# Two sixteenths of the relation weights moved from TensorE to VectorE, and five target one-hots made in one comparison

## What is computed

```python
def rgcn_gate_layer(x, row, col, edge_type, basis, att, gate_w, root, bias):
    w = jnp.einsum('rb,bio->rio', att, basis)      # att 2x30, basis 30x512x512
    x_j = x[col]
    msgs = []
    for r in range(2):
        gate = jax.nn.sigmoid(x_j @ gate_w[r, :, 0])
        msgs.append(gate[:, None] * x_j @ w[r])
    msg = jnp.where((edge_type == 0)[:, None], msgs[0], msgs[1])
    agg = jax.ops.segment_sum(msg, row, num_segments=x.shape[0])
    return agg + x @ root + bias
xn = _layernorm(x)
h = relu(rgcn_gate_layer(xn, ..., basis1, ...)); gnn = rgcn_gate_layer(h, ..., basis2, ...)
x = x + gnn + mix(xn)
x = x + ffn(_layernorm(x))
```

## Time and profile before

| | us |
|---|---|
| three runs | 502.63, 501.56, 502.21 (median 502.21) |
| the profiled execution | 500.15 |
| its span, first to last instruction | 498.4 |
| PE busy | 456.5 (92%) |
| DVE busy | 218.0 (44%) |
| POOL busy | 177.7 (36%) |
| ACT busy | 166.8 (33%) |
| mean granted TensorE clock | 0.987 of full speed |

### The profile page before, as it was taken

How to read it: one execution, slowest core, us unless ns; L and a number is a source line. 1 busy time by engine, 2 the same in 40 slices (tenths; PEclk the granted TensorE clock), 3 DMA queues, 4 the chain that set the end, 5 groups by cost and what they waited for, 6 DMA issues and landing times.

```text
span 498.4 us, 7432 instructions
## 1 busy us (share of the span) xinstructions
PE 456.5 (92%) x2602; PEld 321.5 (65%) x2602; DVE 218.0 (44%) x527; ACT 166.8 (33%) x365; POOL 177.7 (36%) x201
## 2 busy tenths in 40 slices
PE   2799799979999999798999999999999999999993
PEld 2344356768765665466667788777777877775772
DVE  5779981322262626553313002333002658853445
ACT  2799763322220111831205004225006360133320
POOL 3101200055230541199061790622404625940522
PEclk9999999999999999999999999999999999999986
DMA  5999999868999978964910816040002193999646
GB/s 126 380 427 417 429 423 362 345 249 311 369 399 412 383 256 322 422 256 179 315 47 2 250 44 252 1 108 1 5 1 64 42 336 101 272 343 359 209 156 196
DMA packets 38788, 119.27 MB, mean 239 GB/s; under 512 B 7050, under 2 KB 7111, under 8 KB 30302
## 3 DMA queue, kind: packets, MB, share of 16 engines
q1 hardware_dynamic: 33406, 111.30, 59.8%
q0 software_dynamic: 3360, 3.86, 3.2%
q10 hardware_dynamic: 1984, 3.61, 1.9%
HBM read 103.92 MB, written 14.82 MB: 238 GB/s over the span
## 4 chain that ended last, share of the span: by engine, by line
PE 75%; DMA 7%; issue 5%; DVE 3%; ACT 3%; POOL 2%; SPq 2%; DVEq 1%; POOLq 0%; ACTq 0%
PE ps L1637 14%; PE ps L1639 13%; PE ps L1638 13%; PE ps L1661 9%; PE ps L1996 9%; DMA ring<-in_L_gnn_basis_dram 4%; PE ps L1722 3%; DMA y_dram<-ybuf 2%; PE ps L2131 2%; PE ps L2121 2%; PE ps L1841 2%; ACT h_tmp L1374 1%; PE ps L1645 1%; POOL piece_lo L746 1%; DMA got<-y_dram,slot_u 1%
## 5 line engine op out<-in xcount | busy, mean ns | idle before, releaser
L1661 PE MATMUL ps<-ring,sel_att 128*32 128x512 f32 x512 | 66.0, 602 | 6.5 <-DMA ring<-in_L_gnn_basis_dram 3.0
L1637 PE MATMUL ps<-piece_hi,ht_hi 128*125 128x512 f32 x140 | 56.1, 401 | 0.8 <-PE ps L1639 0.6
L1097 DVE SCALAR_TENSOR_TENSOR u_lo<-ps,gates,u_hi 125x512 fp32r<-125x512 f32 x20 | 15.0, 751 | 94.1 <-ACT u_hi L1520 94.1
L1638 PE MATMUL ps<-piece_lo,ht_hi 128*125 128x512 f32 x140 | 55.1, 394 | 0.0
L1639 PE MATMUL ps<-piece_hi,ht_lo 128*125 128x512 f32 x140 | 55.1, 394 | 0.0
L745 POOL CAST piece_hi<-piece_raw 128x512 fp32r<-128x512 f32 x28 | 19.8, 707 | 91.9 <-issue 53.7
L746 POOL TENSOR_TENSOR piece_lo<-piece_raw,piece_hi 128x512 fp32r<-128x512 f32 x28 | 37.8, 1350 | 13.4 <-issue 11.2
L947 DVE TENSOR_SCALAR oh_n<-iota_n,keys 125x626 f16<-125x626 f16 x100 | 37.8, 378 | 8.1 <-PE ps L1722 6.1
L1996 PE MATMUL ps<-u_hi,cf 125*125 125x512 f32 x100 | 39.9, 399 | 1.3 <-PE ps L1639 1.3
L1996 PE MATMUL ps<-u_lo,cf 125*125 125x512 f32 x100 | 39.4, 394 | 0.0
L1722 PE MATMUL ps<-oh_n,oh_m 125*128 125x313 f16 x200 | 31.4, 314 | 4.0 <-DVE oh_m L948 3.9
(11 more groups left out here) (334 smaller groups left out, 929.7 us busy)
## 6 DMA issues: line engine op xcount, KB each, us to landing
ring<-in_L_gnn_basis_dram SPq DMA_DIRECT2D x64, 1024.0 KB, 8.0
w_home<-in_L_ffn_W_sp_dram SPq DMA_DIRECT2D x27, 256.0 KB, 6.5
rel_dram<-stag SPq DMA_DIRECT2D x16, 256.0 KB, 7.9
w_raw<-rel_dram SPq DMA_DIRECT2D x8, 512.0 KB, 6.8
w_fq<-in_L_ffn_W_fq_dram SPq DMA_DIRECT2D x2, 2048.0 KB, 10.7
y_dram<-ybuf ACTq DMA_DIRECT2D x13, 256.0 KB, 4.5
piece_raw<-in_L_mix_Wkqv_dram SPq DMA_DIRECT2D x3, 1024.0 KB, 9.4
x_dram<-stag SPq DMA_DIRECT2D x1, 3072.0 KB
```

The costliest lines, as they stand in the source:

```text
L1097: dve.scalar_tensor_tensor(out=u_lo[l][:, t, :], in0=ps[0:TP, u_bank(i), :], scalar=gates[:, t, r:r + 1], in1=u_hi[l][:, t, :].bitcast(F32 ...
L1637: pe.matmul(target, a_hi, b_hi, start=first, stop=False, skip_group_check=skip)
L1638: pe.matmul(target, a_hi, b_lo, start=False, stop=False, skip_group_check=skip)
L1661: last = pe.matmul(ps[32 * c:32 * c + 32, rel_bank(ch), :], sel_att[:, ch // CHUNKS, g].rearrange("p r q -> p (r q)"), ring[slot][:, c * D ...
```

## The change

Two things change.

First, PE makes only 14 chunks (56 parts). The last two chunks of the second layer, 128 of its 512 input rows, are summed on DVE. For that SP loads the rows of those two chunks in 60 DMAs of 128 KB, into the four `ring` buffers, 64 partitions each (`load_for_vector`): bases 0 to 15 as the last four parts are used on PE, bases 16 to 29 as DVE uses up the first. DVE adds them up in `stag` (`sums`), two relations x 30 bases = 60 instructions of 128 x 512, both inputs and the output in SBUF; `SUMS` gives the order, the two relations in turn for bases 0 to 15, then relation 0 and relation 1 one after the other for the rest. They stand in DVE's list like this: two ahead of each of the five `W2` tiles, three ahead of `gate_row`, six behind it, two behind each `u_lo` of relation 0, and the remaining 31 between relation 0 and relation 1. Each sum waits for its buffer, and for the sum before it on the same relation. The storing and reading back of the second layer's weights is split by relation. ACT no longer copies chunks 14 and 15. SP loads `root2` and `x_again` at other places in its list.

Second, the five `oh_m` of a group are made by one comparison of 125 x 640 elements with broadcast operands.

```diff
-PARTS = 2 * CHUNKS * NG
+V_CHUNKS = 2
+P_CHUNKS = 2 * CHUNKS - V_CHUNKS
+PARTS = P_CHUNKS * NG
...
+            def load_for_vector(turn, s):
+                if turn == 0:
+                    sp.wait_ge(basis_used, PARTS - 4 + s + 1)
+                else:
+                    sp.wait_ge(basis_used, PARTS + s + 1)
+                for b in V_OF[s]:
+                    if b // 16 == turn:
+                        for c in range(V_CHUNKS):
+                            sp.dma_start(ring[s][c * QI * KT:(c + 1) * QI * KT, b % 4 * D:(b % 4 + 1) * D],
+                                         basis_v[b, CHUNKS - V_CHUNKS + c]).then_inc(basis_in[s], 16)
+
+            def store_sum(r):
+                sp.wait_ge(rel_evac, P_CHUNKS + r + 1)
+                for c in range(V_CHUNKS):
+                    sp.dma_start(rel_dram[1][:, r, :, CHUNKS - V_CHUNKS + c, :].rearrange("t q n -> q t n"),
+                                 stag[c * QI * KT:(c + 1) * QI * KT, r, :]).then_inc(rel_out[r], 16)
+
+            def read_second(r):
+                if r == 0:
+                    sp.wait_ge(rel_out[1], 16 * (P_CHUNKS // 2))
                     sp.wait_ge(split_done, PIECE["rel1_1"] + 1)
+                sp.wait_ge(rel_out[r], 16 * (P_CHUNKS // 2 + V_CHUNKS))
                 for t in range(KT):
-                    sp.dma_start(w_raw[:, t, :, :], rel_dram[l][t].rearrange("r q c n -> (q c) r n")
-                                 ).then_inc(rel_back[t], 16)
+                    sp.dma_start(w_raw[:, t, r, :], rel_dram[1][t, r].rearrange("q c n -> (q c) n")).then_inc(rel_back[t], 16)
...
+            load_for_vector(0, 0)
+            load_for_vector(0, 1)
+            store_chunk(P_CHUNKS - 2)
+            load_for_vector(0, 2)
+            load_for_vector(0, 3)
+            store_chunk(P_CHUNKS - 1)
+            load_piece("root2")
             sp.wait_ge(hT_t, NT)
             for a, b in ROWS:
                 sp.dma_start(x_again[a:b, :, :], x.rearrange("(t p) n -> p t n", p=TP)[a:b]).then_inc(x_in, 16)
-            read_relations(1)
+            for s in range(4):
+                load_for_vector(1, s)
+            for r in range(REL):
+                store_sum(r)
+                read_second(r)
...
                         for h in range(TB):
-                            at = tile + (s * TB + h)
-                            dve.tensor_scalar(oh_n[:, s, h, :], iota_n[:], keys[:, 0, bass.ds(at, 1)], None, ALU.is_equal)
-                            last = dve.tensor_scalar(oh_m[:, s, h, :], iota_m[:, j, :], keys[:, 1, bass.ds(at, 1)], None, ALU.is_equal)
-                        last.then_inc(one_hot, 1)
+                            dve.tensor_scalar(oh_n[:, s, h, :], iota_n[:], keys[:, 0, bass.ds(tile + (s * TB + h), 1)], None, ALU.is_equal)
+                        dve.tensor_tensor(oh_m[:, s], iota_m[:, j, :].unsqueeze(1).to_broadcast([TE, TB, REL * WN]),
+                                          keys[:, 1, bass.ds(tile + s * TB, TB)].unsqueeze(2).to_broadcast([TE, TB, REL * WN]),
+                                          ALU.is_equal).then_inc(one_hot, 1)
...
-            for t in range(NT):
+            SUMS = [(b, r) for b in range(16) for r in range(REL)] + [(b, r) for r in range(REL) for b in range(16, BASES)]
+            summed, last_of = [0], [0, 0]
+
+            def sums(count):
+
+                for b, r in SUMS[summed[0]:summed[0] + count]:
+                    s, turn_, target = b // 4 % 4, b // 16, stag[:, r, :]
+                    dve.wait_ge(basis_in[s], 16 * (V_AT[s] + V_CHUNKS * len([a for a in V_OF[s] if a // 16 <= turn_])))
+                    source, factor = ring[s][:, b % 4 * D:(b % 4 + 1) * D], att_all[:, r * BASES + b:r * BASES + b + 1]
+                    if b == 0:
+                        dve.wait_ge(rel_out[r], 16 * (P_CHUNKS // 2))
+                        step = dve.tensor_scalar(target, source, factor, None, ALU.mult)
+                    else:
+                        dve.wait_ge(dve_own, last_of[r])
+                        step = dve.scalar_tensor_tensor(out=target, in0=source, scalar=factor, in1=target, op0=ALU.mult, op1=ALU.add)
+                    step.then_inc(dve_own, 1)
...
+            for t in range(NT):
+                sums(2)
                 dve.wait_ge(w2_mm, t + 1)
...
             def messages(l):
+                if l == 0:
+                    sums(3)
                 dve.wait_ge(gate_mm, l + 1)
                 dve.tensor_copy(in_halves(gate_row[:]), ps[0:2 * REL, 0:2, 0:HALF]).then_inc(gate_row_ready, 1)
+                if l == 0:
+                    sums(6)
                 dve.wait_ge(gates_ready, l + 1)
...
+                        if l == 0 and r == 0:
+                            sums(2)
+                    if a == 0:
+                        sums(len(SUMS) - summed[0])
...
             for t in range(NT):
-                if t == 2:
-                    evac_relation(14)
                 split_transposed(t, t)
...
             turn_xn(0)
-            relation_parts(1)
...
                 if t + 1 < NT:
                     turn_xn(t + 1)
-                relation_parts(1)
...
                 if l == 0:
-                    relation_parts(PARTS - part[0])
+                    assert part[0] == PARTS
                     pe.wait_ge(xm_ready, 3)
```

More of the change, by code:

```diff
@@ L319, in gnn_mix_ffn @@
         w_in, router_in = sem("w_in"), sem("router_in")
[L320 to L323, removed]
+        w2_in, W2_SEEN = [w_in, edges_in, att_in, smalls_in, rel_back[2]], [16, 48, 32, 176, 48]
+        w1_fq_in, W1_FQ_SEEN, w1_moved, w1_moved_dve = rel_back[0], 48, sem("w1_moved"), sem("w1_moved_dve")
+        V_AT = [WIDE // 8 + (PARTS - WIDE) // 4] * 4
+        V_OF = [[b for b in range(BASES) if b // 4 % 4 == s] for s in range(4)]
+        RING_SEEN = [V_AT[s] + V_CHUNKS * len(V_OF[s]) for s in range(4)] + [3] * 4
+        y_out, Y_SEEN = (basis_in[0:3], basis_in[3:8]), [[16 * RING_SEEN[i] for i in r] for r in (range(3), range(3, 8))]
+        w2_fq_in, W2_FQ_SEEN = rel_back[1], 48
         k_hi_done = sem("k_hi_done")
@@ L476, in rel_bank @@
         def rel_bank(ch):
-            return 3 + ch % 2 if ch < 2 * CHUNKS - 2 else 3
+            return 3 + ch % 2 if ch < P_CHUNKS else 3
         def y_buf(b, i):
@@ L552, in _ @@
                 load_part(i)
-            piece_after = {11: "k", 24: "q", 27: "v", 30: "Wo", 34: "W1", 40: "W2", 50: "root1", 62: "root2"}
+            piece_after = {11: "k", 24: "q", 27: "v", 30: "Wo", 34: "W1", 40: "W2", 50: "root1"}
             chunk = 0
@@ L556, in _ @@
                 load_part(i)
-                while chunk < 2 * CHUNKS and i >= min(NG * chunk + (12 if NG * chunk + 12 <= WIDE else 9), PARTS - 1):
+                while chunk < P_CHUNKS - 2 and i >= min(NG * chunk + (12 if NG * chunk + 12 <= WIDE else 9), PARTS - 1):
                     store_chunk(chunk)
@@ L1079, in rest_of_transposed @@
                                   ht_hi[:, :, t * TP:(t + 1) * TP].bitcast(F32), ALU.subtract).then_inc(hT_ready, 1)
+            SUMS = [(b, r) for b in range(16) for r in range(REL)] + [(b, r) for r in range(REL) for b in range(16, BASES)]
[12 more added lines that the diff above has]
+                    step.then_inc(dve_own, 1)
+                    n[0] += 1
+                    last_of[r] = n[0]
+                    if b < 16 and b % 4 == 3 and r == REL - 1:
+                        dve.wait_ge(dve_own, n[0])
+                        dve.sem_inc(basis_used, 1)
+                    if b == BASES - 1:
+                        dve.wait_ge(dve_own, n[0])
+                        dve.sem_inc(rel_evac, 1)
+                summed[0] += count
             for t in range(NT):
+                sums(2)
                 dve.wait_ge(w2_mm, t + 1)
```

33 lines of the change are left out of this document (18 added, 15 removed).

## The result

The changed kernel takes **512.56 us** (median of 4 runs, 511.37 to 514.8) against 502.42 for the kernel before in the same comparison: ratio **1.0206**, 95% interval 1.0166 to 1.0246. It is slower by 10 us. The forecast was 502.4 us, with a range up to 505.5. The profiled execution took 511.37 us, its span is 509.6 us, 11.2 more than before.

A forecast was written before the change was run, and what follows sets the result against it. PE, busy 92% of the span, was taken as the path, the question being whether DVE's new work fits its idle time. -6.4 + 2.7 + 4.2 - 0.3 = +0.2 us gave 502.4 us by the median, range 496.5 to 505.5.

The forecast's parts named there:

- the batch: DVE's sums between message tiles 4 and 7: through too late for PE's tile 7, loss 4.2 us (3.7 to 4.5).
- what PE saves: Relation parts taken off PE around the `W2` tiles and gate logits: 5.9 to 6.6 us together, 6.4 taken.
- the four parts: Parts removed from between PE's `W2` tiles: 5.0 us saved, at least 4.3.
- the last three: Parts removed between the last `W2` tile and the gate logits: 3.12 us long, worth 1.6.
- the 1.5 of the text: PE's wait for the fifth `ht_lo` ahead of the gate logits, until now hidden under parts: about 1.5 us with its signal.
- the part ahead of `W2`: Part before the `W2` product, ending in a 1.39 us idle wait for DVE's `act_lo`: removing it is worth nothing.
- the gates: Nine DVE sums around the gates, alternating with POOL's split of root1: `u_lo` late for message tile 2, loss 2.7 us.
- prices beside POOL: One DVE sum costs 1.34 us under a POOL split, 1.6 under `x_again` additions, 0.65 to 0.79 elsewhere.
- the weights' way back: Relation 0's sum, store, read back and split end 43 us after the root product's start, needed after over 51: no loss.
- The DMA side: Rival: chunk 13's store lands late behind small loads, delaying relation 1's first sum and `W2` tiles: 505 or more, chance 0.18.
- No contention: Rival: DVE's sums cost 0.65 to 0.79 us everywhere, even beside POOL: -6.7 us, 495.5, chance 0.16.
- The one-hots: One comparison for a group's five `oh_m` on DVE: gain 0.3 us, between 0 and 1.

The follow-up runs named there:

- experiment 2: Changed kernel with relation 1's accumulator held in PSUM and copied to SBUF once at the end: 507.5 us, ratio 1.0088 to the kernel before.
- experiment 4: Changed kernel with each accumulating sum on 8 columns instead of 512, all instructions, waits and loads kept: 496.36 us, ratio 0.9887 to the kernel before.
- experiment 5: Kernel before, with the relation part ahead of the `W2` product run behind that product's first tile: 505.66 us, ratio 1.0083.
- experiment 9: Changed kernel with spare matmuls in three PE waits, 4 ahead of `W2`, 6 ahead of message tile 2, 38 ahead of tile 7: 508.65 us, ratio 1.0132.
- experiment 6: Changed kernel with four spare 128x512 matmuls ahead of the `W2` product: ratio 1.0201 to the kernel before.
- experiment 10: Changed kernel with no sums around the gates, a batch of 22, three sums behind each of tiles 5 to 9, four spare products ahead of `W2`: 498.19 us.
- experiment 11: Changed kernel with relation 1 in PSUM, no sums around the gates, batch of 26, last 14 late, four spare products ahead of `W2`: 494.36 us, ratio 0.9839.

## Why the prediction was wrong

Two steps failed: the price of the last 21 sums of the batch, and a term for TensorE's clock that the sum did not have. The forecast was +0.2 us; the profiled span grew by 11.2. Of the 11.0 between them 5.9 are the batch and 6.1 the clock, and what is left, among it the front, made the loss 1.0 smaller.

**Right: what PE saves.** I took 6.4 us in the sum, between 5.9 and 6.6. Measured 5.07 for the four parts (5.0), 1.59 for the last three (1.6), together just above that range. The 1.46 us wait for the fifth `ht_lo` is the 1.5 of the text, and the part ahead of `W2` was worth nothing, as said.

**Right: the gates.** "Loss 2.7 us": measured 2.43, by the mechanism named, sums alternating with POOL's split; `u_lo` of tile 0 was done 13.0 us after the split's start, forecast 13.3.

**Right: prices beside POOL.** 1.34 under a split (1.33 to 1.37 measured), 1.6 under the `x_again` additions (1.70). Experiments 2 and 4 showed the cause.

**Wrong: the batch.** "The remaining 21 at 0.75 to 0.79 (most depend on the one before): 34.2 to 35. Loss 4.2 us (3.7 to 4.5)." The idle time was 10.1. Those 21 sums took 21.4 us, not 16: 14 at 0.86, since a sum that needs the one before starts that much later (1.3 us in all), and 7 at 1.33 beside the split of rel2_0 (3.9 us in all). I had asked of the weights' way back only whether it was too late, and put it at 43 us by two transfers of 5.5 us. By that figure the split would have begun 35 us after the root product's start, with the batch just over; store and read back took 5.7 us together instead of 11, POOL started the split at 301.04, 30.8 after, and the very split that relation 0's early sum sets off slowed relation 1's. The rest lies in the first twelve, at 1.37 and 1.70 instead of 1.34 and 1.6 (0.7 us).

**Missing: the clock.** The sum had no term for what TensorE does after it has idled, and experiment 5 shows such a cost in the kernel before, without the change. By the slow tiles it is 1.37 + 1.7 + 3.0 = 6.1 us; taken away alone it is worth 4.6 us of the middle (experiment 9), and 0.7% by the runs, 1.0206 to 1.0132, whose intervals overlap a little. "The part ahead of `W2`: removing it is worth nothing" was right for the start of that product, and wrong behind it: the part had kept PE busy, and without it the first tile cost 1.4 to 2.4 us more (experiment 6, which took that away alone, won only 0.45 of it up to tile 7).

**The other rivals.** The DMA side did not decide: the second sum did wait 2.93 us for chunk 13's store, and PE lost nothing to it. That was right in part by luck. The store was issued at 230.66, not the 228.3 of the prediction: 16 small loads stand ahead of it in SP's list and took 0.63 us each to issue, where I had put a third of a microsecond. It then landed in 2.7 us, not 5.5. And the slow first tile gave DVE time: in experiments 6, 9, 10 and 11, where that tile ran at full clock, PE waited 0.49, 0.49, 1.18 and 0.35 us for `ht_lo` ahead of the third turning. In experiment 4 all of that traffic is present and PE waits for none of it (with a slow first tile too). "No contention" fell with experiment 2. The one-hots gave more than the 0.3 us taken; by the 0.8 us of the first `k` product they lie at the upper end of "between 0 and 1", by the runs' 1.5 us (0.2 to 2.7) perhaps above it: a group of five is 2.19 us long on DVE against 2.30.

**Open.** Which share of 0.9971 is the comparison's and which the clock's chance in the front can't be told closer than 0.2 to 2.7 us. How the 4.6 us divide among the three fills was not measured: only that at `W2` was tried alone with enough products. Each kernel was profiled once, so a stretch of one trace can hold the clock's chance too.

## What to carry to other kernels

Before work goes to an engine with idle time, write down what its neighbour does in each stretch, count also the neighbour's work that the moved work itself releases, and put an accumulator into PSUM where the neighbour reads SBUF. Place such work where its lateness has slack (behind the last tiles here), not in one batch ahead of a hand-over: the version with the 60 sums lost 10 us as first written, and gained 8 with other places, a PSUM accumulator and four spare products. And when small work is taken out ahead of a wait on TensorE, look at the granted clock of the product behind it; in experiment 9 spare products in the idle time won back 0.7%.

## What the runs showed of the hardware

- **Half clock after short waits.** In all seven executions with 2.26 to 2.60 us of idle ahead of the `W2` product, its first matmuls ran at 1.2 GHz, and tile 0 took 4.25 to 5.26 us; in all six with 1.28 to 1.39 us they ran at 2.4 GHz, and the tile took 2.86 to 2.90 us. Ahead of message tiles 2 and 7 it was the same: behind the five waits of 2.38 to 2.44 us the tile took 4.11 to 4.45 us, behind the three of 1.02 to 1.32 us the clock stayed.
- **The same wait, either level.** Ahead of the first `k` product at 111 PE idles 2.0 to 3.3 us in every execution; in most the clock stayed at 1.00 behind it, in four it fell (0.91 from 110 to 130). Behind a wait of 1.42 us that ends between 205.8 and 209.4, equally long in all, the clock fell in six of the thirteen (0.89 from 200 to 215) and stayed at 1.00 in seven. So the waits above don't give a length below which the clock is safe. Together this moves the start of the `W2` product between 229.2 and 234.0, so single executions differ by 1% in stretches that no edit touched. Ratios over many runs, or the middle stretch alone, are to be compared.
- **Two prices of one instruction.** A 128x512 sum: 0.86 apart alone, 1.33 to 1.37 beside a cast and subtraction of SBUF, 1.70 beside additions of two SBUF inputs. With the accumulator in PSUM it was 0.73 to 0.76 long in all 58 cases (experiments 2 and 11), beside splits and additions too.
- **The wait does not shrink with the instruction.** On 8 columns instead of 512 the same instruction took 0.22 us in the median, and still up to 1.28 us beside POOL (experiment 4).
